# Per-language adapter with layer norm: first products kept further ahead, low part of h on GpSimd, other load order

## What is computed

```python
w1 = W1[language_ids]; w2 = W2[language_ids]
h = jnp.einsum('bsh,bha->bsa', hidden_states, w1) + b1[language_ids][:, None, :]
h = jax.nn.relu(h)
adapted = jnp.einsum('bsa,bah->bsh', h, w2) + b2[language_ids][:, None, :]
x = hidden_states + adapted
mean = jnp.mean(x, axis=-1, keepdims=True)
var = jnp.mean(jnp.square(x - mean), axis=-1, keepdims=True)
normed = (x - mean) * jax.lax.rsqrt(var + LN_EPS)
return normed * gamma[language_ids][:, None, :] + beta[language_ids][:, None, :]
```

## Time and profile before

| | |
|---|---|
| time, median of 3 | 325.74 us (325.51 to 326.59) |
| the profiled execution's own time | 325.01 us |
| its span | 323.3 us |
| busy: PE, DVE | 298.4 us (92%), 308.6 us (95%) |
| busy: ACT, POOL | 240.5 us (74%), 186.0 us (58%) |
| DMA | 75.69 MB, mean 234 GB/s |

### The profile page before, as it was taken

The page is one execution under the profiler, slowest core; times in us unless marked ns, Lnnn a source line. Parts: engine busy times, 40 slices in busy tenths (PEclk is TensorE's granted clock), DMA queues, the critical chain, the costliest instruction groups (busy, mean ns, idle before and its releaser), DMA issues. The chain is left out here.

```text
span 323.3 us, 8131 instructions
## 1 busy us (share of the span) xinstructions
PE 298.4 (92%) x2199; PEld 270.8 (84%) x2200; DVE 308.6 (95%) x679; ACT 240.5 (74%) x605; POOL 186.0 (58%) x217
## 2 busy tenths in 40 slices
PE   2549999999999999999999999999999999999961
PEld 2139899999999999999999999999999999999940
DVE  5878999999999999999999999999999999999996
ACT  4937678777787777877778777787777877778752
POOL 2960764566655566555665556655566555665553
PEclk9968999999999999999999999999999999999997
DMA  4999988666777667766677666776667666433324
GB/s 160 305 354 428 379 297 262 243 228 237 253 240 233 233 221 259 242 225 231 217 252 240 233 233 218 260 245 217 235 219 262 231 228 235 156 132 133 130 109 152
DMA packets 41711, 75.69 MB, mean 234 GB/s; under 512 B 2253, under 2 KB 7404, under 8 KB 41542
## 3 DMA queue, kind: packets, MB, share of 16 engines
q1 hardware_dynamic: 41571, 75.04, 68.2%
q10 hardware_dynamic: 99, 0.14, 0.2%
HBM read 41.62 MB, written 33.55 MB: 233 GB/s over the span
## 5 line engine op out<-in xcount | busy, mean ns | idle before, releaser
L295 POOL TENSOR_TENSOR x_io<-x_io,beta_all 128x512 f32<-128x512 f32 x128 | 161.5, 1284 | 0.0
L403 PE MATMUL ps_h<-w_all,x_T 128*128 x1024 | 143.2, 283 | 0.0
L403 PEld LDWEIGHTS ps_h<-w_all,x_T 128*128 128x128 f32 x1024 | 125.7, 193 | 1.5
L342 ACT ACTIVATE cut<-ps_y,row_sum 128x512 bf16<-128x512 f32 x128 | 87.9, 687 | 22.2 <-PE ps_y L430 22.2
L573 DVE SCALAR_TENSOR_TENSOR x_io<-ps_y,rstd,x_io 128x512 f32<-128x512 f32 x128 | 90.2, 747 | 2.5 <-DVE rstd L565 0.3
L320 ACT COPY x_T<-ps_T 128x512 f32<-128x512 f32 x128 | 74.0, 578 | 23.5 <-PE ps_T L395 23.4
L560 DVE SCALAR_TENSOR_TENSOR ps_y<-ps_y,mean,gamma_all 128x512 f32<-128x512 f32 x128 | 90.7, 753 | 0.7 <-ACT cut L342 0.4
L395 PE MATMUL ps_T<-identity,x_io 128*128 128x128 f32 x512 | 78.6, 277 | 10.7 <-DMA x_io<-in_x 10.7
L292 POOL TENSOR_TENSOR mean<-row_sum,over_h 128x2 f32<-128x2 f32 x64 | 13.0, 203 | 124.6 <-DVE ps_y L541 113.7
L541 DVE SCALAR_TENSOR_TENSOR ps_y<-x_io,b_all 128x512 f32<-128x512 f32 x124 | 83.0, 710 | 0.0
L395 PEld LDWEIGHTS ps_T<-identity,x_io 128*128 128x128 f32 x512 | 63.2, 143 | 20.1 <-issue 11.6
(11 more groups left out here) (60 smaller groups left out, 171.4 us busy)
## 6 DMA issues: line engine op xcount, KB each, us to landing
x_io<-in_x SPq DMA_DIRECT2D x64, 512.0 KB, 4.4
out<-x_io SPq DMA_DIRECT2D x63, 512.0 KB, 3.0
x_io<-in_L_cond_W SPq DMA_DIRECT2D x5, 512.0 KB, 7.2
w_all<-in_L_cond_W SPq DMA_DIRECT2D x5, 512.0 KB, 8.7
b_all<-in_L_cond_b SPq DMA_DIRECT2D x1, 2560.0 KB, 15.1
out<-x_io SPq DMA_DIRECT2D x2, 256.0 KB, 2.0
x_io<-in_L_cond_gamma SPq DMA_DIRECT2D x1, 60.0 KB
x_io<-in_L_cond_beta ACTq DMA_DIRECT2D x1, 60.0 KB
```

Of the source, the lines that this page charges most:

```text
L295: nc.gpsimd.tensor_tensor(x_slot(t), x_slot(t), of_lang(beta_all, langs[b]), ALU.add)\
L342: nc.scalar.activation(squares[:, t % 2, :], ps_y[t % Y_BANKS][:, :], ACT.Square, scale=-float(H), bias=stat(row_sum, t), accum_out=stat(s ...
L403: last = nc.tensor.matmul(part, x_T[:, t % 4, c, :], w1_all[:, bass.ds(lang, 1), c, :].rearrange("p o a -> p (o a)"), start=False, stop=(c ...
```

## The change

The new source moves line numbers: L430 becomes L462, L403 L434, L541 L568, L295 L320.

1. **Lead.** FIRST is 5. At step 5 TensorE does the second products of pairs 0 and 1; the lead in steps is then 4, from step 15 on 3 and from step 25 on 2, by a step with two second products each time (EASE = 10, LAST = 2). The list is given by `ended` and `heads`.
2. **Low part of h.** ScalarE copies `ps_hT` twice, as it is into `h_T` and rounded into `h_high`; GpSimd subtracts them, both in SBUF, into `h_low`. It does so between its two beta additions of a pair. VectorE's `low_h` is gone.
3. **b1.** Both bias matmuls of a pair stand ahead of its sixteen others.
4. **ScalarE's step** has the high part of h ahead of both copies of x.
5. **Loads.** One chunk of W2 goes ahead of W1 where there were two, then x and W2 alternate, and b2 comes behind x of pair 6. beta's rows are loaded ahead of b1's. VectorE copies nine of the twenty spread tiles where it copied four.

```diff
+    def ended(p):
+        return 0 if p < FIRST else p + 1 - max(LAST, FIRST - START - (p - FIRST) // EASE)
+    def heads(p):
+        return range(ended(p - 1), ended(p))
+    def low_with(n):
+        for p in range(FIRST, PAIRS):
+            if heads(p)[0] == n - 1:
+                return p - 1
+        return PAIRS - 1 if n == ended(PAIRS - 1) + 1 else None
...
-    by_act = [n for n in range(2 * L) if n not in (L, L + 2, L + 4, L + 6)]
-    by_dve = [n for n in range(2 * L) if n not in by_act]
+    by_dve = [n for n in range(3, 2 * L) if n % 2 == 1]
+    by_act = [n for n in range(2 * L) if n not in by_dve]
...
+            def low_h(p):
+                pool.wait_ge(h_T_ready, p + 1)
+                pool.wait_ge(h_high_ready, p + 1)
+                nc.gpsimd.tensor_tensor(flat(h_low[:, p % H_PAIRS, :, :]), flat(h_T[:, p % 2, :, :]),
+                                        flat(h_high[:, p % H_PAIRS, :, :]).bitcast(F32), ALU.subtract).then_inc(h_low_ready, 1)
...
                 for b in range(2):
                     t = 2 * n + b
                     nc.gpsimd.tensor_tensor(x_slot(t), x_slot(t), of_lang(beta_all, langs[b]), ALU.add)\
                         .then_inc(x_beta_ready, 1)
+                    if b == 0 and p is not None:
+                        low_h(p)
...
+            for p in range(FIRST - 1):
+                low_h(p)
+            mean_and_beta(0, None)
+            for n in range(1, PAIRS):
+                mean_and_beta(n, low_with(n))
...
+                if p >= 2:
+                    act.wait_ge(h_low_ready, p - 1)
+                nc.scalar.copy(flat(h_T[:, p % 2, :, :]), pair_of(ps_hT)).then_inc(h_T_ready, 1)
                 nc.scalar.copy(flat(h_high[:, p % H_PAIRS, :, :]), pair_of(ps_hT)).then_inc(h_high_ready, 1)
...
             for p in range(PAIRS):
-                if p >= FIRST:
-                    n = p - FIRST
+                for n in heads(p):
```

More of the change, by code:

```diff
@@ L16 @@
 H_PAIRS = 6
-FIRST = 3
+FIRST = 5
+LAST = 2
+START = 1
+EASE = 10
 EARLY = 2
-W2_AHEAD = 2
+W2_AHEAD = 1
 def build(nc, x, ids, w1, b1, w2, b2, gamma, beta, out):
@@ L363, in _ @@
             copy_x(1)
-            for n in range(L):
+            for n in by_act:
                 copy_spread(n)
[L366 to L380, removed]
+            for p in range(FIRST):
+                copy_x(2 * p + 2)
+                if p > 0:
+                    high_h(p - 1)
+                high_w2(p)
+                copy_x(2 * p + 3)
+                copy_h(p)
             for p in range(FIRST, PAIRS):
-                square_pair(p - FIRST)
+                for n in heads(p):
+                    square_pair(n)
                 step(p)
-            square_pair(PAIRS - FIRST)
+            square_pair(ended(PAIRS - 1))
             high_h(PAIRS - 1)
-            for n in range(PAIRS - FIRST + 1, PAIRS):
+            for n in range(ended(PAIRS - 1) + 1, PAIRS):
                 square_pair(n)
@@ L397, in turn_x, with h_sums, put_b1 @@
                 last.then_inc(x_turned, 1)
+            def h_sums(t):
+                return pair_of(ps_h)[:, (t % 2) * A:(t % 2 + 1) * A]
+            def put_b1(p):
+                for b in range(2):
+                    nc.tensor.matmul(h_sums(2 * p + b), of_lang(pick, langs[p][b]), b1_parts[:, :],
+                                     start=(b == 0), stop=False, skip_group_check=True)
             def first_product(t, lang):
-                part = pair_of(ps_h)[:, (t % 2) * A:(t % 2 + 1) * A]
-                nc.tensor.matmul(part, of_lang(pick, lang), b1_parts[:, :], start=True, stop=False)
                 for c in range(C):
-                    last = nc.tensor.matmul(part, x_T[:, t % 4, c, :],
+                    last = nc.tensor.matmul(h_sums(t), x_T[:, t % 4, c, :],
                                             w1_all[:, bass.ds(lang, 1), c, :].rearrange("p o a -> p (o a)"),
-                                            start=False, stop=(c == C - 1))
+                                            start=False, stop=False, skip_group_check=True)
                 if t % 2 == 1:
@@ L477, in _ @@
                         put_b2(2 * p + b, langs[p][b])
-            for n in range(PAIRS - FIRST, PAIRS):
+            for n in range(ended(PAIRS - 1), PAIRS):
                 for b in range(2):
                     second_product(2 * n + b, langs[n][b])
-                if n == PAIRS - FIRST:
+                if n == ended(PAIRS - 1):
                     turn_h(PAIRS - 1)
@@ L576, in _ @@
             dve.wait_ge(over_h_ready, 2)
-            for n in range(W2_AHEAD):
-                mean_of_w2(n)
             for n in by_dve:
@@ L596, in _ @@
             seed_early(1)
-            low_h(1)
             dve.wait_ge(s_b2, 16)
-            def norm_and_seed(n, p):
+            for n in range(PAIRS):
                 scale_pair(n, langs[n])
```

67 lines of the change are left out of this document (28 added, 39 removed).

## The result

The changed kernel takes **345.63 us** (median of 5 runs, 345.37 to 347.26). Five runs of the kernel before, made beside it, give the same 325.74 as the runs shown above. The ratio is 1.061, with a 95% interval of 1.058 to 1.064: slower by 6%, 19.9 us. Forecast were 343.1 us, with 0.71 for slower. The profiled execution took 347.26 us, the longest of the five, with a span of 345.3 us.

The account below looks back on a forecast made before the run. TensorE was taken to bound the kernel before (4.49 us a pair, VectorE 4.42). Seed at 46.6, 51.6 for the next, turns of 278.5 to 330.1, end 10.6: span 340.7, time 343.1 us, range 338 to 348.

Parts of the forecast that it names:

- The turn of seeds, additions and subtraction: Steady loop: seed, means, addition, subtraction, addition, seed takes 4.66 us a pair, more than TensorE's 4.49.
- the single row of 19.66: VectorE's L524 in the earlier trace: began in effect 0.19 us before GpSimd's instruction ended; the same was assumed for seeds.
- Seeds not shut out: Rival for the loop: beta additions do not delay seeds, TensorE sets the pace at 4.44; 323.0 us, chance 0.24.
- Shut out until the very end: Rival for the loop: a seed begins only when the addition has ended, 4.85 a turn; 354.1 us, chance 0.13.
- Seeds slipping ahead: Rival for the loop: waiting seeds mostly go before the second beta addition, no change; about 325.7 us, chance 0.05.
- The pairs without a subtraction: Changes of the lead: pairs 13 and 24 have no subtraction, two turns of 4.09 us instead of 4.66.
- The start: Before the loop: first second product at 40.6 us instead of 33.96, pair 2's second seed at 46.6, pair 3's at 51.6.
- The 1.3 us for a beta addition between the last two low parts of W2: Start: GpSimd's first beta addition gets in between, with ScalarE's late high parts +1.3, moving the first second product to 40.6.
- 6.0 us were counted: Start: from the first second product to pair 2's second seed, 5.41 without low part, 6.0 with pair 4's subtraction between.
- The end: From pair 63's second seed: 3.05 to the subtraction's end, 3.29 to the inverse, 4.3 to the span's end; 10.6 us.
- The sum: Whole kernel: span 340.7 us, 17.4 more than before; 343.1 us as a median.
- Counted as hidden: ScalarE's second copy (26 us more, 267 of some 340) and paired b1 (0 to 0.06 a step) cost or save nothing.

Follow-up runs that it names:

- experiment 1: Changed kernel with the loop's seeds reading one SBUF tile instead of two, so b2 is left out of all but the first two pairs: 324.89 us.
- (2): Kernel before plus one spare 256-column GpSimd subtraction between the two beta additions of each pair: 339.34 us, ratio 1.042.
- (3): Kernel before plus the same spare GpSimd subtraction, cut to 64 columns: 325.62 us, ratio 1.001.
- experiment 5: Kernel before with only the two b1 bias matmuls of a pair put together: 322.20 us, ratio 0.990; run again later, 323.48 us, ratio 0.993.
- experiments 6 to 10: Changed kernel with low parts all on VectorE (326.54 us), alternating (338.02), halved (327.19); kernel before with paired b1, lead 3 to 2 (324.10), earlier low part (325.04).
- experiment 4: Changed kernel with GpSimd's subtraction behind both beta additions instead of between them: 353.44 us, ratio 1.085.
- experiment 7: Changed kernel with low parts of odd pairs on VectorE and those of even pairs on GpSimd: 338.02 us, ratio 1.036.
- experiment 9: Kernel before with b1 together, low part right behind the inversion, ScalarE's high part first, lead going from 3 to 2 at step 33: 324.10 us.
- experiment 10: Kernel before with paired b1 and lead going from 3 to 2 at step 33, the low part there made one pair earlier: 325.04 us.

## Why the prediction was right

**The turn of seeds, additions and subtraction: right, 4.66 against 4.70.** Term by term the rows gave 0.87, 0.14, 1.24 for 1.25 and 0.69 for 0.70 (the subtraction itself takes 0.73, where about 0.74 was forecast). What was off is the seed's start: 0.13 ahead of the addition's end, not the 0.19 that was read from the single row of 19.66. 58 turns of 0.045 more are 2.6 us. The cause is shown from three sides: without the second SBUF input it goes away (experiment 1), in the kernel before the subtraction alone brings it (2), and with a short one it does not come (3).

**The rivals.** *Seeds not shut out* fell with the first seed's 1.29 us; experiment 1 is this case made real, and gave 324.9 for the rival's 323.0, its stall included; 1.5 us of its trace lie in the stretch at the lower clock. *Shut out until the very end* priced the turn at 4.85, and 0.13 is nearer to the 0.19 read than to nothing. The Trainium skill, "SBUF — State Buffer", section "Who interferes with whom", says which instructions contend, and that the loser is blocked for the whole instruction, the latter in its sentence on VectorE's modes with two ports. As to which contend, all traces here agree, from the earlier trace rows to experiment 1; as to how long, the recorded times show 0.13 us less. *Seeds slipping ahead* was not seen in the steady loop.

**The pairs without a subtraction: a term too small in this trace.** They were counted with 4.09 and nothing after. The turn is 4.08, but the next is 6.06 behind pair 13, and 5.46 behind pair 24 (second seed to second seed, by where they began in effect): together 2.1 us more than two turns of 4.70. GpSimd's timeline around pair 13, from the subtraction in pair 12's turn on, then VectorE's:

```profile
98.57 0.73 POOL L309 TENSOR_TENSOR h_low<-h_T,h_high 128x256 fp32r<-128x256 f32 x1 [2.98 <-ACT h_high L370]
...
100.64 2.98 POOL L320 TENSOR_TENSOR x_io<-x_io,beta_all 128x512 f32<-128x512 f32 x2
```

```profile
100.64 0.75 DVE L600 SCALAR_TENSOR_TENSOR x_io<-ps_y,rstd,x_io 128x512 f32<-128x512 f32 x1 [0.34 <-POOL x_io L320]
101.31 1.18 DVE L568 SCALAR_TENSOR_TENSOR ps_y<-x_io,b_all 128x512 f32<-128x512 f32 x1
...
102.41 1.76 DVE L568 SCALAR_TENSOR_TENSOR ps_y<-x_io,b_all 128x512 f32<-128x512 f32 x1
```

Pair 12's subtraction waits for ScalarE's high part, so the additions behind it run late, and pair 14's seeds and pair 13's additions then take turns, each waiting out the other; the second seed, recorded at 102.41 with 1.76 us, began in effect at 103.44. The prediction had looked at GpSimd's list there, and not at when its input is ready. But part of the lateness is the clock of this execution. TensorE's timeline and the window behind it (the third number from the end is the granted clock):

```profile
93.56 0.77 PE L462 MATMUL ps_y<-w_high,h_high 128*128 x1 [3.06 <-DVE ps_y L568]
...
94.00:99.00 5.00, 5.00 (x20) 4.28 (x20) 4.96 (x13) 2.99 (x8) 1.86 (x3) 0.50 0.68 232
```

TensorE had stood for 3.06 us, waiting for pair 12's seeds; its granted clock was 0.50 from 92.6 to 99.4, and the second product took 2.70 us instead of 1.48. The high part started 4.49 us behind that product's start, where an undisturbed step has 2.94 (105.19 to 108.13). Behind the change of the lead at step 25 it was the same, a wait of 3.06 and a granted clock of 0.50 from 147.2 to 150.6, and the high part 3.53 behind. What these two turns take at full clock no trace here shows.

**The start: terms off by 1 us that nearly cancel.** The first second product stands at 39.47 for 40.6. Of its terms, x of pair 1 was right (TensorE's first wait for it ends at 20.58, forecast 20.4). The 1.3 us for a beta addition between the last two low parts of W2 was wrong: the two ran undisturbed and GpSimd was the one that waited.

```profile
37.90 1.43 DVE L557 SCALAR_TENSOR_TENSOR w_low<-x_io,w_neg_mean,w_high 128x512 fp32r<-128x512 f32 x2 [0.58 <-ACT w_high L355]
```

```profile
38.25 0.47 POOL L317 TENSOR_TENSOR mean<-row_sum,over_h 128x2 f32<-128x2 f32 x1
38.68 3.04 POOL L320 TENSOR_TENSOR x_io<-x_io,beta_all 128x512 f32<-128x512 f32 x2
```

The means took 0.47 for 0.20 and the two additions 3.04 for 2.53. So the first second product came 1.1 us early. From there to pair 2's second seed 6.0 us were counted:

```profile
45.80 1.76 DVE L568 SCALAR_TENSOR_TENSOR ps_y<-x_io,b_all 128x512 f32<-128x512 f32 x1
```

It was shut out, and began in effect at 46.84, 7.4 us behind: the inverse had come 3.75 us behind the product instead of 3.29, pair 4's subtraction held up the first seed, and pair 1's second addition the second. That addition had been priced at 0.9, but a pair later; pair 3's second seed, with nothing in its way, stands 4.09 behind in effect, at 50.93 for 51.6. The three misses (1.1 early, 1.4 late, 0.9 early) leave 0.7 early. That they are small together is luck. b2 was not waited for, as forecast.

**The end: 11.15 for 10.6.** Pair 63's second seed starts at 334.15. The last turn on VectorE:

```profile
340.33 0.76 DVE L587 SCALAR_TENSOR_TENSOR ps_y<-ps_y,mean,gamma_all 128x512 f32<-128x512 f32 x1 [0.29 <-ACT cut L375]
341.00 0.16 DVE L592 RECIPROCAL rstd<-std 128x2 f32<-128x2 f32 x1
```

From the last second product's start (337.35) the inverse follows after 3.65, not 3.29, and that product starts 0.24 behind the subtraction's end.

**The sum.** In span: -0.7 at the start, +2.6, +2.1 and +0.55, 4.6 in all, on the forecast 340.7, is the 345.3 measured. In medians the forecast misses by 2.5. The difference is that this profiled execution lies 1.6 above its median, while that of before lay 0.7 below (and its time is 2.0 above its span, where that of before had 1.7). The other four executions took 1.4 to 1.9 us less than this one, at a mean granted clock of 0.976 to 0.986 for its 0.970. So much of the 2.1 behind pairs 13 and 24 may be this execution's low clock and not the forecast's term; that is an estimate from those times, since only this execution has a trace.

**Counted as hidden, rightly:** ScalarE's second copy (353 ns each, ACT's busy time 256.2, forecast up to 267), and b1 together, whose 0.05 a step lay within 0 to 0.06 and shows only where TensorE sets the pace (experiment 5). That the lead costs nothing from step 25 on was right for the steady turn there, and wrong, in this trace, for the turn at which it changes.

## What to carry to other kernels

Before work is moved to an idle engine, draw the turn in which it lands: here GpSimd was 42% idle, but 0.70 us between two of its instructions came between two seeds of VectorE, through SBUF and not through any semaphore. Where several engines are nearly balanced, don't average over turns: each turn takes the longest of its bounds, and what a change at one place costs once (a step with two second products, a late start) was not caught up in experiments 6 to 10. Before two traces are compared to within 1 or 2 us, look at the granted clock in both: a half-rate stretch can look like a longer stall. Look for small savings on the engine that sets the pace first: two bias matmuls side by side brought 0.7 to 1%, and no shorter or longer lead added to it.

## What the runs showed of the hardware

- A VectorE instruction with two SBUF inputs that meets a GpSimd one with two SBUF inputs starts in effect 0.13 us before the recorded end of that one, in turn after turn (0.17 for a second seed in experiment 4, 0.19 in the one row of before), and its wait is counted as its own busy time: 1.29 us for 0.69. It works the other way too: a subtraction of 0.73 us that met a seed is recorded with 1.25. VectorE's busy share was 95% before and after, although the 64 low parts were gone and the span was 22 us longer.
- GpSimd's operations with two SBUF inputs, 128 partitions: 0.20 us for 2 columns, 0.32 for 64, 0.46 for 128, 0.73 for 256, 1.28 for 512.
- A low part right behind an inversion costs VectorE 0.20 us a pair and not 0.33: VectorE's own turn is 4.29 with it (experiment 7), 4.09 without. The next instruction then starts 0.07 behind the inversion's start (73.60 and 73.67), where without it the one that needs the inverse starts 0.19 behind (209.09 and 209.28).
- In experiment 9 TensorE's granted clock fell to a mean of 0.89 from 171 to 186 us; the matmuls behind the 1.96 us wait start 0.43 us apart where others start 0.23 apart, near the lower of the clock's two levels, 1.2 for 2.4 GHz. In experiment 10 a wait of 1.82 at the same place had no such effect. The changed kernel had two such stretches, at a granted clock of 0.50, around the ends of its two waits of 3.06, and experiment 1 one behind a wait of 2.31. What decides between them these runs do not show.
